# A gather that adds onto the edge features in SBUF, in place of a buffer and a VectorE addition

## What is computed

```python
h_proj = jnp.einsum('nd,rde->rne', h, relation_weight)   # 32 relations
t_r = h_proj[etype, src]
h_r = h_proj[etype, dst]
att = jnp.sum(t_r * jnp.tanh(h_r + efeat), axis=-1)
seg_max = jax.ops.segment_max(att, dst, num_segments=N)
att_exp = jnp.exp(att - seg_max[dst])
denom = jax.ops.segment_sum(att_exp, dst, num_segments=N)
msg = h[src] * (att_exp / denom[dst])[:, None]
h_nb = jax.ops.segment_sum(msg, dst, num_segments=N)
```

## Time and profile before

| | |
|---|---|
| median of 3 runs | 14831.56 us (14820.45 to 14836.97) |
| span of the profiled execution, first to last instruction | 14826.2 us |
| busy in that span: POOL | 11251.3 us (76%), 9773 instructions |
| DVE | 4329.1 us (29%) |
| ACT | 2086.7 us (14%) |
| PE | 1074.3 us (7%) |

### The profile page before, as it was taken

One profiled execution on the slowest core, in us unless ns is written; L12 is line 12 of the kernel. 1 busy time (PEld: TensorE's weight loads), 2 busy tenths in 40 slices (PEclk: granted clock), 3 DMA queues, 4 the chain that ended last, 5 costly groups with the idle time before them and its releaser, 6 DMA issues. The chain is left out here.

```text
span 14826.2 us, 41742 instructions
## 1 busy us (share of the span) xinstructions
PE 1074.3 (7%) x8029; PEld 821.2 (6%) x8029; DVE 4329.1 (29%) x4363; ACT 2086.7 (14%) x1546; POOL 11251.3 (76%) x9773
## 2 busy tenths in 40 slices
PE   7300000000000000000000000003000000000001
PEld 3100000000000000000000000003000000000001
DVE  3333333333333333333333333334111111111112
ACT  3100000000000000000000000002222222222221
POOL 1587877888887777888777788885777777777776
PEclk9655555555555555555555555555555555555555
DMA  9522222222222222222222222221111111111111
GB/s 409 200 55 55 54 54 54 52 55 54 55 54 55 53 53 55 54 55 55 55 55 53 53 54 55 55 52 35 48 46 48 48 47 47 48 46 48 46 48 42
DMA packets 405795, 947.81 MB, mean 64 GB/s; under 512 B 188612, under 2 KB 191716, under 8 KB 392852
## 3 DMA queue, kind: packets, MB, share of 16 engines
q0 software_dynamic: 306272, 416.74, 13.5%
q1 hardware_dynamic: 63508, 322.91, 5.9%
q10 hardware_dynamic: 36000, 208.02, 3.5%
HBM read 527.08 MB, written 419.93 MB: 64 GB/s over the span
## 5 line engine op out<-in xcount | busy, mean ns | idle before, releaser
L834 POOL DMA_INDIRECT gd<-table,idx_d x3125 | 3847.8, 1231 | 952.8 <-issue 952.8
L831 POOL DMA_INDIRECT gs<-table,idx_s x3125 | 3761.3, 1204 | 981.2 <-issue 952.5
L1007 POOL DMA_INDIRECT gy<-ytab,idx x3125 | 3347.1, 1071 | 1048.1 <-issue 997.2
L892 DVE TENSOR_TENSOR gd<-gd,ef 128x1600 f32<-128x1600 f32 x125 | 229.4, 1835 | 5865.0 <-DMA gd<-table,idx_d 5865.0
L1040 DVE TENSOR_TENSOR_SCAN run<-keep,add 128x1664 f32<-128x1664 f32 x125 | 453.1, 3625 | 3464.1 <-ACT keep L1064 3382.7
L941 ACT ACTIVATE gd<-gd 128x1600 f32<-128x1600 f32 x125 | 192.0, 1536 | 7374.7 <-issue 3773.2
L972 PE MATMUL hist_s<-hi_s,lo_s 128*128 128x98 bf16 x3125 | 507.5, 278 | 8965.7 <-DVE hi_d L882 8965.7
L972 PEld LDWEIGHTS hist_s<-hi_s,lo_s 128*128 128x128 bf16 x3125 | 433.4, 141 | 8989.4 <-DVE hi_d L882 8989.4
L1062 ACT COPY add<-gy 128x1600 f32<-128x1600 f32 x125 | 400.5, 3204 | 2930.6 <-DMA gy<-ytab,idx 2930.6
L949 ACT COPY rowbuf<-run 128x1625 f32<-128x1625 f32 x125 | 411.7, 3293 | 716.5 <-DVE run L914 716.5
L973 PE MATMUL hist_d<-hi_d,lo_d 128*128 128x98 bf16 x3125 | 508.1, 278 | 0.0
(11 more groups left out here) (182 smaller groups left out, 2877.1 us busy)
## 6 DMA issues: line engine op xcount, KB each, us to landing
table<-rows SPq DMA_DIRECT2D x98, 2048.0 KB, 14.1
sums<-rowbuf ACTq DMA_DIRECT2D x125, 825.0 KB, 3.4
ef<-in_edge_attr_dram SPq DMA_DIRECT2D x125, 800.0 KB
sums<-rowbuf ACTq DMA_DIRECT2D x125, 800.0 KB
gs<-table,idx_s POOLq DMA_INDIRECT x3125
gd<-table,idx_d POOLq DMA_INDIRECT x3125
gy<-ytab,idx POOLq DMA_INDIRECT x3125
ytab<-y SPq DMA_DIRECT2D x7, 448.0 KB
```

Source lines behind the costliest of these rows:

```text
L831: pool.indirect_dma_start(out=gs[:, s, g, :], out_offset=None, in_=table, in_offset=bass.IndirectOffsetOnAxis(ap=idx_s[:, s, g:g + 1], axi ...
L834: pool.indirect_dma_start(out=gd[:, s, g, :], out_offset=None, in_=table_half, in_offset=bass.IndirectOffsetOnAxis(ap=idx_d[:, s, g:g + 1] ...
L1007: pool.indirect_dma_start(out=gy[:, s, g, :], out_offset=None, in_=ytab, in_offset=bass.IndirectOffsetOnAxis(ap=idx[:, s, g:g + 1], axis=0 ...
```

## The change

The buffer `gd` goes. The destination's rows are gathered straight into `ef[:, s]`, each DMA adding its rows to the edge features that lie there. So POOL has to wait until those features have landed before it issues a chunk's gathers. VectorE's addition and its semaphore `tanh_arg` go: ScalarE takes the tanh in `ef` as soon as the gathers have landed, and the next load into `ef` waits for `arg_free`, which VectorE raises when its sum over the features (the `tensor_reduce`) has read the slot.

```diff
-            gd = sb(c2, "gd", [P, 2, G, D])
...
-                        sp.wait_ge(tanh_arg, 2 * i + 1)
+                        sp.wait_ge(arg_free, 2 * i + 1)
                         load(2 * i + 2, 0)
...
-                    def gather(c, s):
+                    def gather(c, s, i):
                         pool.wait_ge(slot_ready, c + 1)
+                        pool.sem_inc(pool_past, 1)
+                        pool.wait_ge(ef_in[s], 16 * (i + 1))
                         pool.sem_inc(pool_past, 1)
...
-                                out=gd[:, s, g, :], out_offset=None, in_=table_half,
-                                in_offset=bass.IndirectOffsetOnAxis(ap=idx_d[:, s, g:g + 1], axis=0)).then_inc(gd_in[s], 16)
+                                out=ef[:, s, g, :], out_offset=None, in_=table_half,
+                                in_offset=bass.IndirectOffsetOnAxis(ap=idx_d[:, s, g:g + 1], axis=0),
+                                compute_op=ALU.add).then_inc(gd_in[s], 16)
...
-                    SETUP, PER_CHUNK = 6, 13
+                    SETUP, PER_CHUNK = 6, 12
...
-                        dve.wait_ge(ef_in[s], 16 * (i + 1))
-                        dve.wait_ge(gd_in[s], 16 * G * (i + 1))
-
-                        nc.vector.tensor_tensor(gd[:, s, :, :], gd[:, s, :, :], ef[:, s, :, :], ALU.add).then_inc(tanh_arg, 1)
-
                         dve.wait_ge(gs_in[s], 16 * G * (i + 1))
                         dve.wait_ge(tanh_done, c + 1)
-                        link.then(nc.vector.tensor_tensor(gd[:, s, :, :], gd[:, s, :, :], gs[:, s, :, 0:D], ALU.mult))
-                        link.then(nc.vector.tensor_reduce(att[:, :], gd[:, s, :, :], AX.X, ALU.add))
+                        link.then(nc.vector.tensor_tensor(ef[:, s, :, :], ef[:, s, :, :], gs[:, s, :, 0:D], ALU.mult))
+                        nc.vector.tensor_reduce(att[:, :], ef[:, s, :, :], AX.X, ALU.add).then_inc(arg_free, 1)
+                        dve.wait_ge(arg_free, c + 1)
...
-                        act.wait_ge(tanh_arg, c + 1)
-                        nc.scalar.activation(gd[:, s, :, :], gd[:, s, :, :], ACT.Tanh).then_inc(tanh_done, 1)
+                        act.wait_ge(gd_in[s], 16 * G * (i + 1))
+                        nc.scalar.activation(ef[:, s, :, :], ef[:, s, :, :], ACT.Tanh).then_inc(tanh_done, 1)
```

More of the change, by code:

```diff
@@ L797, in gnn_program @@
             slot_ready = sem(c2, "slot_ready")
-            tanh_arg, tanh_done = sem(c2, "tanh_arg"), sem(c2, "tanh_done")
+            tanh_done, arg_free = sem(c2, "tanh_done"), sem(c2, "arg_free")
             exp_arg, exp_done = sem(c2, "exp_arg"), sem(c2, "exp_done")
@@ L817, in _ @@
                     with sp.Fori(0, PAIRS - 1) as i:
-                        sp.wait_ge(tanh_arg, 2 * i + 1)
+                        sp.wait_ge(arg_free, 2 * i + 1)
                         load(2 * i + 2, 0)
-                        sp.wait_ge(tanh_arg, 2 * i + 2)
+                        sp.wait_ge(arg_free, 2 * i + 2)
                         load(2 * i + 3, 1)
-                    sp.wait_ge(tanh_arg, CHUNKS - 2)
+                    sp.wait_ge(arg_free, CHUNKS - 2)
                     load(CHUNKS - 1, 0)
@@ L834, in gather @@
                             pool.indirect_dma_start(
-                                out=gd[:, s, g, :], out_offset=None, in_=table_half,
-                                in_offset=bass.IndirectOffsetOnAxis(ap=idx_d[:, s, g:g + 1], axis=0)).then_inc(gd_in[s], 16)
+                                out=ef[:, s, g, :], out_offset=None, in_=table_half,
+                                in_offset=bass.IndirectOffsetOnAxis(ap=idx_d[:, s, g:g + 1], axis=0),
+                                compute_op=ALU.add).then_inc(gd_in[s], 16)
                     with pool.Fori(0, PAIRS) as i:
-                        gather(2 * i, 0)
-                        gather(2 * i + 1, 1)
-                    gather(CHUNKS - 1, 0)
+                        gather(2 * i, 0, i)
+                        gather(2 * i + 1, 1, i)
+                    gather(CHUNKS - 1, 0, PAIRS)
                 @block.vector
```

## The result

The changed kernel takes 16637.64 us (median of 4 runs) against 14827.98 us: a ratio of 1.1219, 95% interval 1.1206 to 1.1233. The forecast was slower, by 474 us; it is slower by 1,810, outside the range of 14,700 to 16,150 us and between its upper end and the 17,020 us of rival (c).

The account below looks back on a forecast made before the run. POOL's list of 6,250 gathers was taken to bound the edge stage. Dearer adding gathers, +562 us, less 88 for the removed addition, give +474 on 14,832: 15,306 us, range 14,700 to 16,150 (the forecast's own from 14,885).

Parts of the forecast that it names:

- rival (c): On POOL an adding gather costs the whole 0.81 us more, 17,020 us, or the DMA engines become the bound; chance 0.12.
- the addition and the product: VectorE's removed addition gives POOL 0.80 us a chunk; the product's hold goes from 0.96 to 0.82; 118 us in all.
- The moved waits: POOL's new wait for the features' load, the later load issue, and ScalarE's and VectorE's waits: together 0.
- part 2: The 3,125 destination gathers on POOL now add: 0.20 us more each, 625 us, of which 562 show.
- the same formula: 22.5 of 25 adding gathers a chunk show their extra price, over 125 chunks, less 88 us for the removed addition.
- its bounds: POOL's hold behind VectorE's product, by where it falls in POOL's beat: 0.44 to 1.69 us, 1.06 in the middle.
- (a): An adding gather costs POOL no more than a copying one: 14,714 us, by the beat 14,666 to 14,823; chance 0.36.
- (b): An adding gather costs POOL a trifle, 0.042 us, at which gain and loss cancel; chance 0.05.

## Why the prediction was wrong

Its reading of the kernel was right. POOL's gathers are the stage, VectorE's two-input instructions hold them up, and the addition and the product were sized well: 118 us forecast for a copying gather, 133 measured; 0.82 us for the product, 0.79 measured. The moved waits cost nothing, as said; the load lands 4.4 us after its issue by the page of the changed kernel.

The step that failed is part 2, "with half of it by the row the addition costs 0.81 x 1/2 x 1/2 = 0.20 us". The price is 0.60. Its reasoning was that an addition adds only to what goes by the row. So it put a fixed price of the adding form at nothing, without a reason, and that is where some 0.43 us of the 0.60 are. The row's part is 0.17 us (128 x 1.35 ns), near the forecast's 0.20, but that is luck: a copying gather's rows are cheap, 944 - 867 = 77 ns for 96 rows, so the row's part of its 0.81 us is about 0.1 and not a half, and by the forecast's own rule the addition would have cost 0.05 us. The forecast price was a third of the true one. With 0.604 in the same formula, 22.5 x 125 x 0.604 - 88 = 1,611 us. The rest to 1,802 is 125 us of the copying gathers' tail, and holds that shrank by 210 us where the formula takes off 88 + 2.5 x 125 x 0.604 = 277: the product's came out at 1.50 us a chunk, near the upper end of its bounds and not in the middle.

The rivals: (a) and (b), with no price and with 0.042 us, are refuted by 1,548 ns. The first half of (c), like the forecast, put the price in POOL's own work, which is right; its 0.81 us is 0.21 too high. Its second half, the DMA engines as the bound, is refuted by the 20.8% and by the run with half the bytes. The Trainium skill's rule in "Collectives: The Full Stack", "The bandwidth ceiling: the fold count and why AG ≠ RS ≠ AR", that the reduce step of a collective reads twice where a copy reads once and so runs at half the rate, points the way that the engines went here (0.37 to 0.42 us for 0.23). They had slack, and rows that travel alone could cost the same, so no run shows the rule itself. It doesn't give POOL's price if a list of twice the reads costs by the row, since most of the price doesn't.

The Trainium skill's remark in "SBUF — State Buffer", "Who interferes with whom", that `tensor_tensor` had not stalled descriptor generation, is contradicted by these runs for indirect gathers. Its rule itself, that two SBUF inputs are what matters, is borne out by each mask, addition and product that was given one input in PSUM.

What stays open: what the fixed 0.43 us is spent on, since no view shows the inside of a gather. And why TensorE's matmuls and VectorE's wait for them stall when POOL is hardly held up.

## What to carry to other kernels

Where GpSimd issues many small indirect DMAs, count what one of them costs the issuing engine before giving it more to do: here 125 additions of 1.83 us, hidden for all but 0.80 us each, were bought with 3,125 dearer gathers. To take a VectorE instruction out of GpSimd's way it was enough here to give it one operand in PSUM. Take the holds away step by step, since another engine may live on them.

## What was not expected of the hardware

- An adding indirect gather of 128 rows costs GpSimd 0.60 us more than a copying one, of 64 rows 0.52, of 32 rows 0.47: by estimate 0.43 whatever its rows, and 1.3 to 1.4 ns a row; the gather behind it is 0.04 us longer.
- A copying gather's price is nearly all fixed: 867 ns for 32 rows, 944 for 128.
- With three or four of the masks in PSUM the histogram's matmuls, which need 4 us a chunk, come one every 2.8 us once some 36 have run, in about one chunk of five, with no releaser in the profile, and VectorE's wait for them ends up to 88 us after the last. With two, or with more matmuls a chunk but all masks in SBUF, they don't. That the engine's instructions arrive too slowly while gathers go out without pause is an argument, not shown.
